# One kernel, four chained layers: the first tile's low rank taken in fp32 from w2's rows as they stand, and b's rows permuted by transfers inside SBUF

## The reference, cut to what matters

```
x = x + L0(x)            # modulated dense layer
x = x + L1(x)            # tanh RNN over the 128 steps, H = 512
# L2: ae = layernorm(cond); h = gelu(ae @ w1 + b1); xw = h @ w2 + b2
x_a, x_b = split(xw, 2, axis=-1)      # each reshaped to (32, 512, 8)
layer = base[None] + einsum('bdr,bkr->bdk', x_a, x_b)   # rank 8, one matrix per batch
x = x + (x + einsum('btc,bco->bto', x, layer))
x = x + L3(x)            # LSTM over the 128 steps, H = 512, gates 2048
```

## Time and profile before

| | us |
|---|---|
| median of 3 runs | 1130.18 |
| lowest and highest | 1129.91, 1130.26 |
| the profiled execution, its own time | 1131.51 |
| its span, first to last instruction | 1129.7 |
| TensorE matmul busy | 1092.5 |
| VectorE busy | 885.4 |
| ScalarE busy | 426.1 |
| mean granted TensorE clock | 0.995 |

### The profile page before, as it was taken

The page is one execution under the profiler, slowest core; times in us unless marked ns, Lnnn a source line. Parts: engine busy times, 40 slices in busy tenths (PEclk is TensorE's granted clock), DMA queues, the critical chain, the costliest instruction groups (busy, mean ns, idle before and its releaser), DMA issues.

```text
span 1129.7 us, 65707 instructions
## 1 busy us (share of the span) xinstructions
PE 1092.5 (97%) x30300; PEld 741.5 (66%) x30300; DVE 885.4 (78%) x2786; ACT 426.1 (38%) x1034; POOL 16.7 (1%) x48
## 2 busy tenths in 40 slices
PE   5779999999999999999999999999999999999997
PEld 3436666676766667676766767666766766676657
DVE  7888878777787877778777777887777778777765
ACT  5884333333333333333333333333333333333322
POOL 1000000000000000000000000000000000000000
PEclk9989999999999999999999999999999999999999
DMA  9991000000000000000000000000000000000000
GB/s 337 404 379 40 23 23 3 22 23 23 22 22 23 6 20 22 23 22 22 23 9 16 23 23 22 23 23 14 12 23 22 23 22 22 13 4 13 13 13 22
DMA packets 24644, 51.96 MB, mean 46 GB/s; under 512 B 4160, under 2 KB 4288, under 8 KB 23344
## 3 DMA queue, kind: packets, MB, share of 16 engines
q1 hardware_dynamic: 23936, 47.49, 11.9%
q10 hardware_dynamic: 432, 0.26, 0.1%
HBM read 39.36 MB, written 8.39 MB: 42 GB/s over the span
## 4 chain that ended last, share of the span: by engine, by line
PE 91%; DMA 4%; DVE 3%; issue 1%; ACT 1%; ACTq 0%; DVEq 0%
PE ps_gates L1563 57%; PE ps_l L1502 8%; PE ps_x L1502 7%; PE ps_l L1615 7%; PE ps_rnn L1615 7%; DMA ring<-in_hw 3%; PE ps_lr L1502 2%; PE ps_z L1532 1%; PE ps_l L1563 1%; DVE big L840 1%; DMA rows<-in_ln_b 1%; PE ps_gates L1471 1%; DVE gates_ring L1126 0%; PE ps_l L1449 0%; DVE b_lo L840 0%
## 5 line engine op out<-in xcount | busy, mean ns | idle before, releaser
L1563 PE MATMUL ps_gates<-big,rows 128*32 128x512 f16 (+1 forms) x6144 | 358.5, 376 | 1.2 <-ACT rows L525 1.2
L1563 PE MATMUL ps_gates<-big,lstm_h 128*32 128x512 f16 (+1 forms) x6144 | 348.9, 376 | 1.0 <-DVE lstm_h L1159 1.0
L1563 PEld LDWEIGHTS ps_gates<-big,lstm_h 128*32 128x32 f16 x6144 | 163.9, 97 | 156.2 <-DVE lstm_h L1159 2.4
L1563 PEld LDWEIGHTS ps_gates<-big,rows 128*32 128x32 f16 x6144 | 161.9, 97 | 141.1 <-issue 1.3
L1126 DVE SCALAR_TENSOR_TENSOR gates_ring<-ps_gates,tile_un,rows 128x256 f32<-128x256 f32 x252 | 110.6, 480 | 94.2 <-PE ps_gates L1563 94.2
L666 ACT ACTIVATE gates_ring<-gates_ring 128x256 f32<-128x256 f32 x128 | 53.4, 417 | 257.6 <-DVE gates_ring L1126 257.6
L1502 PE MATMUL ps_l<-xs,w_hi 128*128 128x128 f16 x1024 | 80.2, 222 | 0.8 <-issue 0.6
L1502 PE MATMUL ps_x<-x,base_hi 128*128 128x128 f16 x1024 | 78.1, 219 | 0.0
L525 ACT ACTIVATE xs<-xsT,tile_s 128x512 f16<-128x512 f32 x32 | 23.1, 721 | 114.6 <-DVE xsT L853 111.1
L1502 PEld LDWEIGHTS ps_l<-xs,w_hi 128*128 128x128 f16 x1024 | 63.1, 100 | 3.1 <-issue 1.6
L1502 PEld LDWEIGHTS ps_x<-x,base_hi 128*128 128x128 f16 x1024 | 62.5, 98 | 1.4 <-issue 1.4
(11 more groups left out here) (221 smaller groups left out, 1710.9 us busy)
## 6 DMA issues: line engine op xcount, KB each, us to landing
ring<-in_hw SPq DMA_DIRECT2D x16, 1024.0 KB, 14.7
xT_sb<-in_xT SPq DMA_DIRECT2D x32, 256.0 KB, 2.8
outT<-late SPq DMA_DIRECT2D x32, 256.0 KB, 2.0
big<-in_wx SPq DMA_DIRECT2D x5, 1024.0 KB, 14.6
big<-in_wh SPq DMA_DIRECT2D x5, 1024.0 KB, 14.3
big<-in_w SPq DMA_DIRECT2D x1, 1024.0 KB, 5.8
big<-in_hw SPq DMA_DIRECT2D x1, 1024.0 KB, 13.4
late<-in_base SPq DMA_DIRECT2D x1, 1024.0 KB, 14.3
```

The costliest lines, as they stand in the source:

```text
L1563: last = nc.tensor.matmul(by_chunk_of_gate(bank[B * j:B * j + B, columns]), of_step, tile_columns(w, j)[:, gates], start=start, stop=stop, ...
```

## The change

It has five parts.

1. The first tile's low rank. `z(0)` becomes `first_z`: a is the stationary operand and z comes out as rank and batch on partitions, tokens on columns (24 matmuls of 128 columns). `first_mask` masks and scales it in one fp32 operation. `first_low_rank(q)` multiplies b's rows as `w2_unit` left them (fp32, no split) with it, and adds the products in the same PSUM banks to which `first_base` wrote x2 . base (four banks, one for each output chunk). `first_x3` on ScalarE moves the sum out. `move_b`, `row_picks`, and tile 0's `zm_high`, `zm_low`, `low_rank_share` and `x3_first` go.
2. For later tiles b's rows are put in order by sixteen transfers from SBUF to SBUF (`b32`, in a slot of `ring` that is free by then), issued by SP between the last load of x's first tiles and b3's transfers. `b_high` and `b_low` read them, and stand behind x2's split now.
3. The batches stand in another order in the rows of w2: `aeT` is written in the order half, group, batch. `by_rank` shrinks to (k, q, c), so a's columns lie in the order rank, half, group, batch. `z(a)` for later tiles takes its 64 columns through `columns_of_group`, every 32nd for the rank.
4. `l1(8)` goes ahead of `w2_unit(13)`.
5. The first iteration of the main loop (i = 2) has an order of its own: L0's input scales, `xs` and `xs_low` of tile 3, which stood ahead of the loop, stand in it, `l0(3)` and `x1(3)` go later, `gates_x(2)` ahead of `x3_low_rank(1)`.

```diff
+        b32 = ring[:, 0, 0:2 * D].rearrange("p (h n) -> p h n", h=2)
-            return x.rearrange("p (k g n q j) -> p k q j n g", k=2, g=KC, n=BG, q=2)
+            return x.rearrange("p (k q c) -> p k q c", k=2, q=2)
...
             load_x(XT_RING - 1)
+            for q in range(2):
+                sp.wait_ge(rows_ready, 3 + 2 * q)
+                sp.wait_ge(w2_used, 3 * KC + 1)
+                for j in range(RH):
+                    for half in range(2):
+                        sp.dma_start(b32[RH * q + j:P:RANK, half], b_rows[B * j + BH * half:B * j + BH * half + BH, q])\
+                          .then_inc(mv_b, 16)
             sp.wait_ge(a_ps, 2)
...
+            def first_x3():
+                act.wait_ge(first_scales_ready, 1)
+                for oc in range(KC):
+                    act.wait_ge(first_ps, oc + 1)
+                    last = high(x3T[0][:, oc].rearrange("p t b -> p (t b)"), ps_first[oc][:, 0:TOK], first_un)
+                    if oc % 2 == 1:
+                        last.then_inc(x3_ready, 1)
...
             for i in range(LAG, TILES - 1):
                 a1, c, t, r = i - LAG + 1, i + 1, STEPS * (i - LAG), STEPS * i
                 lstm_sums(t)
+                if i == LAG:
+                    x_magnitude(c, c)
                 lstm_cell(t)
                 rnn_sums(r)
                 lstm_turned(t)
...
                 rnn_out(r)
                 zm_low(a1)
                 lstm_out(t)
-                x1(c)
                 if i == LAG:
-                    x_magnitude(LAG + 2, 0)
-                x3_first(a1)
-                x1_low(c)
+                    tile_scales(c, 1, c)
+                    xs(c)
+                    tile_undo(c, 1, c)
+                    xs_low(c)
+                    sum_links()
+                    gate_scales(a1)
+                else:
+                    x1(c)
+                    x3_first(a1)
+                    x1_low(c)
                 lstm_sums(t + 1)
...
                 lstm_out(t + 1)
+                if i == LAG:
+                    x3_first(a1)
+                    x1(c)
+                    x_magnitude(LAG + 2, 0)
+                    x1_low(c)
                 x3_low(a1)
...
+            def columns_of_group(w, g):
+                return w.rearrange("p (r h g b) -> p g h b r", r=RANK, h=2, g=KC)[:, g]
...
                         for g in range(KC):
-                            last = nc.tensor.matmul(ps_z[B * g:B * g + B, 0:2 * B], of_group(x2_16[:, part, k], g),
-                                                    w[:, k, 2 * B * g:2 * B * g + 2 * B], start=(n == 0 and k == 0),
+                            last = nc.tensor.matmul(ps_z[B * g:B * g + B, 0:2 * B].rearrange("p (h b r) -> p h b r", h=2, b=BQ),
+                                                    of_group(x2_16[:, part, k], g), columns_of_group(w[:, k], g),
+                                                    start=(n == 0 and k == 0),
...
+            def first_z():
+                pe.wait_ge(x2_lo_ready, 1)
+                for q in range(2):
+                    for n, (part, w) in enumerate(((0, a_hi), (0, a_lo), (1, a_hi))):
+                        for k in range(KC):
+                            last = nc.tensor.matmul(ps_z[:, TOK * q:TOK * q + TOK], w[:, k, P * q:P * q + P], x2_16[:, part, k],
+                                                    start=(n == 0 and k == 0), stop=(n == 2 and k == KC - 1))
+                last.then_inc(z_ready, 1)
...
+            def first_low_rank(q):
+                pe.wait_ge(zm_ready, 1)
+                for oc in range(KC):
+                    if q == 0 or oc % 2 == 0:
+                        pe.wait_ge(rows_ready, 3 if q == 0 else 4 + oc // 2)
+                    last = nc.tensor.matmul(ps_first[oc][:, 0:TOK], b_rows[:, q, P * oc:P * oc + P],
+                                            zm_first[:, STEPS * q:STEPS * q + STEPS].rearrange("p t b -> p (t b)"),
+                                            start=False, stop=(q == 1))
+                    if q == 1:
+                        last.then_inc(first_ps, 1)
...
             pe.wait_ge(a_lo_ready, 2)
-            z(0)
+            first_z()
             w2_unit(11)
             rnn(7)
             w2_unit(12)
+            l1(STEPS * LAG)
             w2_unit(13)
-            move_b(0)
+            pe.wait_ge(base_lo_ready, 2)
+            first_base()
             w2_unit(14)
-            pe.wait_ge(base_lo_ready, 2)
-            x3_base(0, (0, 1))
+            first_low_rank(0)
             w2_unit(15)
-            move_b(1)
-            x3_base(0, (2, 3))
-            x3_low_rank(0)
-
-            l1(STEPS * LAG)
+            first_low_rank(1)
...
                 z(a1)
-                l0(c)
-                x3_base(a1, range(KC))
-                x3_low_rank(a1)
-                l1(r + 1)
-                lstm(t + 1)
-                rnn(r + 1)
-                l1(r + 2)
-                gates_x(t + 2)
+                if i == LAG:
+                    x3_base(a1)
+                    l1(r + 1)
+                    gates_x(t + 2)
+                    x3_low_rank(a1)
+                    lstm(t + 1)
+                    rnn(r + 1)
+                    l1(r + 2)
+                    l0(c)
+                else:
+                    l0(c)
+                    x3_base(a1)
+                    x3_low_rank(a1)
+                    l1(r + 1)
+                    lstm(t + 1)
+                    rnn(r + 1)
+                    l1(r + 2)
+                    gates_x(t + 2)
                 gates_x(t + 3, (0,))
                 lstm(t + 2)
```

More of the change, by code:

```diff
@@ L1056, in b_scale, with sum_links @@
                 over_power(s_b, exps[:, 8:9], TOP).then_inc(b_scale_ready, 1)
[L1059 to L1062, removed]
+            def sum_links():
                 dve.wait_ge(b_scale_ready, 1)
[L1064 to L1068, removed]
+                linked(nc.vector.tensor_copy(sum_link[:, 0:1], s_base))
+                linked(nc.vector.scalar_tensor_tensor(sum_link[:, 1:2], s_a, 2.0 ** -Z_SHIFT, s_b, ALU.mult, ALU.mult))
             def gate_scales(a):
@@ L1320, in _ @@
             last_magnitudes()
-            b_scale()
             x3_bound()
-            b_low()
             gate_scales(0)
-            x_magnitude(XT_RING - 1, XT_RING - 1)
-            x3_first(0)
             wh3_low(2, 1)
             x3_low(0)
+            b_scale()
             wh3_low(3, 0)
@@ L1332, in _ @@
             low(lstm_h16[:, 1], condT_sb[:], tile_g[:, 0, 1:2], lstm_h16[:, 0]).then_inc(lstm_lo_ready, 1)
-            tile_scales(XT_RING - 1, 1, XT_RING - 1)
-            xs(XT_RING - 1)
             x2_low(1)
-            tile_undo(XT_RING - 1, 1, XT_RING - 1)
-            gate_scales(1)
-            xs_low(LAG + 1)
+            b_low()
             dve.wait_ge(ld_b3, 16 * KC * GATES)
@@ L1483, in turn_a, with split_product @@
                     last.then_inc(a_ps, 1)
-            def move_b(q):
-                if q == 0:
-                    pe.wait_ge(rows_ready, 3)
-                    pe.wait_ge(l0_scaled, LAG + 1)
-                    pe.wait_ge(zm_ready, 1)
-                else:
-                    pe.wait_ge(rows_ready, 5)
-                for half in range(2):
-                    last = nc.tensor.matmul(ps_b[half][:], row_picks[:, q, half], b_rows[:, q], start=(q == 0), stop=(q == 1))
-                    if q == 1:
-                        last.then_inc(b_ps, 1)
-            def split_product(psum, w_parts, x_parts):
+            def split_product(psum, w_parts, x_parts, stop=True):
                 (w_hi, w_lo), (x_hi, x_lo) = w_parts, x_parts
@@ new lines, in first_base, with x3_base @@
+            def first_base():
+                for oc in range(KC):
+                    last = split_product(ps_first[oc][:, 0:TOK], (chunks(base_hi, oc), chunks(base_lo, oc)),
+                                         [[x2_16[:, part, k] for k in range(KC)] for part in range(2)], False)
+                last.then_inc(base_ps, 1)
+            def x3_base(a):
+                pe.wait_ge(x3_ready, x3_count(a - 1))
+                dense(ps_x3, base_hi, base_lo, x2_16, range(KC)).then_inc(base_ps, 1)
@@ L1756, in _ @@
                 if t == T - LAG * STEPS + 1:
-                    x3_base(TILES - 1, range(KC))
+                    x3_base(TILES - 1)
                 if t == T - LAG * STEPS + 2:
```

123 lines of the change are left out of this document (71 added, 52 removed).

## The result

The changed kernel takes 1164.60 us (median of 5 runs, 1164.41 to 1165.45) against 1130.18 (5 runs beside it, 1129.91 to 1131.24). The ratio is 1.0305, 95% interval 1.0291 to 1.0319: slower, by 34.4 us, where 7.3 were forecast. The profiled execution took 1164.53 us, with a span of 1162.7 (33.0 more than before) and a mean clock of 0.993.

What follows compares the result with a forecast made beforehand. TensorE was taken to bound the kernel after the loads. Head +2.9, clock +0.1 and z's stepped operand +4.3 made +7.3 us on the 1130.2 median, so 1137.5 us, range 1131 to 1150.

Steps and rivals of the forecast that it cites:

- the early part: Work ahead of gates_x(0): shorter first low rank lets gates_x(0) begin at 89.9 against 93.55 us, 3.7 us gained.
- the cost of z: z(1) to z(31) on TensorE: stepped operand doubles a wave's column time, z 0.53 to 0.67 us, 4.3 in all; chance 0.37.
- the sum: Whole kernel: +2.9 for the head, +0.1 for the clock, +4.3 for z, together +7.3 us.
- The prediction's own sign of being wrong: Wrong if b3 lands before 101 us, or a middle iteration keeps its length or grows by over 0.3 us.
- The rival with VectorE's whole time per element: z of later tiles: 113 ns a wave, +0.82 us per z, 25 in all, 1158 us; chance 0.12.
- Where the gain goes: SP: SP's queue: sixteen moves of b's rows at 0.48 us each delay b3, which lands at 103.7 us.
- T0: End of VectorE's wait for b3 ahead of lstm_sums(0), forecast at 103.7 us (bounds 101.6 and 105.6).
- The path from T0: First loop iteration, lstm_sums(0) to lstm(4): lstm(4) at T0 + 30.9 = 134.6 us against 131.69, +2.9 us.
- The clock: Hole ahead of gates_x(2): TensorE then at 1.2 GHz, products 1.5 us longer, 0.8 beside VectorE; counted as 0.1.
- the landmark: lstm(4), at 131.69 us before the change; nothing idles before it, tiles repeat behind it; forecast at 134.6.
- The faster rival: SP's queue: short issues bring T0 before 100.8; with b3 wholly out of the way 1128.1 us; chance 0.08.
- the dear rivals: z's stepped operand costs VectorE's extra per element, 1144.0 us, chance 0.15, or its whole time, 1158, chance 0.12.

Runs made afterwards that it cites:

- two kernels: Changed kernel with GpSimd's grouped copy and b3 ahead of half of b's moves, 1135.57 us; the same with a new first-iteration order, 1133.58 us.
- the first of the three: Changed kernel with a's columns put into group order once by sixteen GpSimd copies, so z reads contiguous columns: 1137.19 us, ratio 1.0067.

## Why the prediction was wrong

- **The direction and the early part were right.** gates_x(0) began at 90.21 (forecast 89.9, before 93.55), lstm(0) at 95.39 (95.1). The four fp32 products of first_low_rank(0) took from 84.81 to 85.90, 0.27 each (0.25). That piece of the head did get 3.3 us shorter.
- **The step that failed is the cost of z**: "If the element needs two steps where it needed one, a wave is 128 columns' time, 56 ns, and z 0.67 ... I take the double time." A wave took 122 ns, z 1.46 to 1.50: +0.93 to +0.97, not +0.14. Alone in the kernel before it cost 28.6 us, where the sum held 4.3. The prediction's own sign of being wrong, an iteration longer by over 0.3 us, came true with 0.85. The rival with VectorE's whole time per element (113 ns a wave, z +0.82, 25 in all, 1158 us) was the nearest, 25 us where 28.6 were measured, and had a chance of 0.12. That it comes near isn't shown to be more than luck: nothing here ties TensorE's read to VectorE's time. The argument against it, "no row of TensorE shows so slow a read", was empty: no row showed any read by TensorE with its elements apart. Whether the 17 ns of room in a wave hid a part can't be told; one slow stream of the four is enough to set the wave.
- **The Trainium skill's rule** (SBUF — State Buffer, Specifications), two hits in a 16-byte line for full bandwidth, pointed the right way. The runs agree with it at the upper end: from one element in 16 bytes on, a further step costs nothing more. At 8 bytes apart a line still has two hits, and z was 0.85 us, not 0.53; there the runs differ from the rule of two hits. The page also says that each change of line costs, and by that alone some cost is expected there. The page has no price, and I had put the likeliest case at the small one.
- **"Where the gain goes: SP" was right in kind and too small.** Sixteen moves at 0.48 us (bounds 0.35 and 0.60) were 0.736 each (11.77/16). Their median is 0.589, and an ordinary one starts 0.63 after the one before, already above the upper bound; two took 1.09 and 1.80, as the earlier trace rows had shown for b3 with 1.34. T0 was 107.8, 4.1 behind 103.7 and outside its bounds. What was wrong: the price was put between the rows of b3's loads and of the output's stores, and a transfer from SBUF to SBUF is dearer for SP than either.
- **"The path from T0" held.** `lstm_sums(1)` at T0 + 9.4 (9.5), `lstm_sums(2)` at T0 + 20.4 (20.4), lstm(4) at T0 + 31.3 (30.9). The head cost +7.45 for 2.9 forecast: 4.1 from T0, 0.4 from the path.
- **The clock** after the hole was 0.50, of its two levels 1.2 GHz, as forecast. gates_x(2) took 4.46 us where 2.76 is usual, 1.7 and not 1.5 more; most of it lay beside VectorE, since the landmark is only 0.4 late against T0. The length of the hole alone doesn't decide it: the hole of 1.52 us ahead of gates_x(0) was followed by full clock here (gates_x(0) and (1) 5.36 us), but by 0.50 in the changed kernel with contiguous z, where the same 96 products took 7.05. The windows of TensorE (length, busy, clock, DMA share, GB/s):

```profile
103.00:109.00 6.00, 1.04 (x53) 0.99 0.41 94
109.00:110.00 1.00, 1.00 (x16) 0.50 0.37 131
...
112.00:113.00 1.00, 1.00 (x20) 0.82 0.00 0
113.00:114.00 1.00, 1.00 (x32) 1.00 0.00 0
```

- **The faster rival had the right mechanism and lacked one bound.** With b3 out of the way it gave T0 = 97.8 and lstm(4) near 129.6. The kernel without moves had T0 98.18 and lstm(4) at 131.70. In the price of that rival I had let TensorE be the bound after T0. It was one up to `lstm_sums(1)`, which waited 2.19 us for it; from there to gates_x(4) VectorE's list of the first iteration was. Only with that list shortened, z contiguous and b3 ahead of half of the moves did lstm(4) come at 129.76, and 1127.75 us against the rival's 1128.1.

What stays open: why GpSimd's copies held VectorE in two kernels and hardly in the first of the three. There the same operation took 0.47 us, and the copies themselves 4.03 and 5.51 us for eight, where they took 2.83 in the other two. That one of the two engines is slowed is seen in all three; what decides which wasn't tried. The Trainium skill (SBUF — State Buffer, Who interferes with whom) says that a VectorE operation with two inputs in SBUF and a GpSimd operation that reads SBUF exclude each other, by a lock held for a whole instruction, and that the order of issue decides who waits. The operation held here has two such inputs (`tile_g` and `link`), so the rows agree with the exclusion. They differ in its length: it waited for a dozen copies of 0.34 us, not for one.

## What to carry to other kernels

A change of layout that saves work once, in the head, puts its price into every use of the operand: here gates_x(0) came 3.3 us earlier, of which nothing was left at the landmark, against 0.9 us in each of 30 iterations on the bound engine. Where the trace has no row of such an access on the engine in question, the dear rivals deserve more than a far end: here the dearest of them came nearest. A single small experiment, one access pattern in the kernel before, would have priced it. And a transfer put ahead of others on a queue costs every one behind it its mean issue time, stragglers included, not its median.

## What the runs showed of the hardware that was not expected

- A moving operand of 64 fp16 elements costs a wave of four products 44 ns in a row, 71 ns with elements 8 bytes apart, and 123 to 130 ns from 16 bytes on, whatever the distance; runs of four neighbours, written to PSUM at a step, cost 65. One such stream of the four is enough: 128 ns.
- Sixteen SBUF-to-SBUF transfers of the kind here took SP 0.589 us each in the median, and 0.736 in the mean from one to the next; b3's sixteen, from memory, 0.432 and 0.539.
- Copies by GpSimd inside SBUF can hold up a VectorE operation on two elements for 4.2 us, until they end. Where nothing slowed them, one copy started 0.32 us after the other on ScalarE and 0.34 on GpSimd.
